# A two-layer graph network on one core: the loads, table stores and first splits ahead of the second product, put in another order

## The chip, the cores and the metric

The kernel runs on one core of one Trainium2 chip. The metric is the device time of one execution in microseconds; the median of three runs is quoted. Everything else is read from one profiled execution.

## The reference

```python
N, F = 4096, 128        # x: [N, F], adj: [N, N], symmetric pattern, non-negative
h = relu(layernorm(x))
d = 1 / sqrt(adj.sum(-1))
z = leaky_relu((d * (adj @ (d * h))) @ W1 + b1, 0.1)
dist = sqrt(max(sq_i + sq_j - 2 z z^T, 0) + 1e-10)
S = where(rank of exp(-dist / 2) in its row < 4, exp(-dist / 2), 0)
d2 = 1 / sqrt((S + adj).sum(-1))
x = x + (d2 * ((S + adj) @ (d2 * h))) @ W2 + b2
h = relu(layernorm(x))
x = x + h @ W_self.T + (adj @ h) @ W_neigh.T + b
```

The adjacency matrix, 64 MB, is multiplied three times. S has four entries in each row, so S @ (d2 * h) @ W2 is a sum of four gathered rows of a table d2 * (h @ W2).

## The kernel before, in words

Rows are kept in 32 tiles of 128, four tiles (U) to a group, eight groups (GROUPS). The adjacency is cut into 64 units of 1 MB (128 partitions x 4 x 512); a unit (g, j) is what group g needs of group j. The first product reads the matrix, transposes the units on VectorE and keeps them in HBM as `at`.

**Search.** Then, for each of 32 tiles, TensorE makes 4096 distances (`distances`, L1259), ScalarE brings them into one of four key buffers (`keys`, which are the four slots of `araw`), and VectorE finds the four best. Tiles go in quads. For three of each quad (`VIA`) VectorE reduces blocks of 64 to their maxima (L988), SyncE stores the keys in HBM (`keys_store`, L440), GpSimd gathers the four best blocks back (`read_blocks`, L501, the gathers at L511), and VectorE searches these candidates (L1010, L1012). The fourth is searched whole (L1001, L1003). GpSimd also adds the first layer's bias to `xs` (L535) between the gathers.

**Between search and second product.** The four values of a row go through a square root and exp (L1034 to L1038), and `dinv` is made of the new row sums (L1041). GpSimd decodes the block places into row indices (L567 to L576). VectorE scales `hw_sb`, the rows of h @ W2 (it lies in two slots of `tr`), by `dinv` into `gw` (`table_part`, L1048; it lies in `zt_lo`), and SyncE stores `gw` in HBM as the neighbour table (L476, four transfers of 512 KB in runs of 512 B). When it has landed (`table_out`), GpSimd gathers from it: 8 groups of 16 indirect transfers of 128 rows (`gather_group`, L578, L588), which go into `zt_lo`, over `gw`. Group g waits until VectorE has used group g-2 (`gath_used`).

**Second product.** It holds one group of accumulations at a time, eight units each. The units lie in a ring of eight places (`ring`, the same memory as the key buffers: two units in each key buffer), loaded by SyncE (`load_unit`, L418, the transfer at L428) as soon as TensorE has used the unit before in that place (`u_used`). Even units are multiplied as they are (`whole_unit`, L1294, 4 matmuls) by `ys` (`second_y`, L1044). Odd units are split: ScalarE casts them into a high part (`split_high`, L755, L761, in one of four places of `ring_hi`, the memory of `tr`), VectorE subtracts to get the low part (`split_low`, L1118, L1122), and TensorE runs three products of each block (L1289 to L1291) with the high and low parts of y, made by ScalarE (`y_hi`, L796) and VectorE (`second_y_low`, L1051). After a group, VectorE adds the gathered rows (`finish_second_a`, L1070, L1080), adds to x, takes the layer norm's statistics, and ScalarE and VectorE make and keep the next h (L781, L784, L1116). On VectorE these stand between the last split of group g+1 and the first of group g+2.

**Third product.** All units are split; group g needs all kept h. GpSimd adds the last bias (L603), which waits for `bias_in`.

The order on each engine is that of the code. The work around the change, on SyncE:

```python
            sp.wait_ge(x_b2, QUADS - 1)          # L462: seven bias additions of GpSimd
            sp.wait_ge(kept, 1)                  # L463: and the eighth
            sp.dma_start(bias[:], ...)           # L464
            for p in range(4):                   # L465
                ...                              # key buffer p stored and searched
                load_unit(0, 2 * p), load_unit(0, 2 * p + 1)
            sp.wait_ge(gw_ready, 1)              # L474
            ...                                  # four table stores, L476
```

Of the kernel before, what the change touches and what calls it, by code (L numbers as in the profile page):

```python
# [31 lines left out]
P = 128  # L32
QD = 4
R = 32
TILES = N // P
U = 4
GROUPS = TILES // U
# [10 lines left out]
QUADS = TILES // 4  # L48
# [3 lines left out]
DMA = 16  # L52


def gnn_kernel(nc, x, adj, W1, b1, W2, b2, W, b, out):
# [12 lines left out]
    table_v = table.rearrange("(q t s) f -> q s t f", q=QD, t=TILES)  # L68
# [3 lines left out]
    with ctx:  # L72
        places = {}

        def sb(name, shape, dt=F32):
            places[name] = -(-nc.sbuf_base // 32) * 32
            return ctx.enter_context(nc.sbuf_tensor(name, shape, dt))
# [4 lines left out]
        def sem(name):  # L82
            return ctx.enter_context(nc.semaphore(name))
# [23 lines left out]
        bias = sb("bias", [P, F])  # L107
# [65 lines left out]
        gw = units_z[1][:].rearrange("p i u (k f) -> p (i u k) f", f=F)  # L173
# [20 lines left out]
        bias_in = sem("bias_in")  # L194
# [42 lines left out]
        x_b2 = sem("x_b2")  # L237
# [20 lines left out]
        gw_ready = sem("gw_ready")  # L258
        table_out = sem("table_out")
# [10 lines left out]
        kept = sem("kept")  # L270
        last_bias = sem("last_bias")
        dinv_done = sem("dinv_done")
# [130 lines left out]
        def _(sp):  # L403
# [55 lines left out]
            with sp.Fori(1, QUADS) as quad:  # L459
                for p in range(VIA):  # L460
                    keys_store(quad, p)
            sp.wait_ge(x_b2, QUADS - 1)  # L462
            sp.wait_ge(kept, 1)  # L463
            sp.dma_start(bias[:], b.partition_broadcast(P)).then_inc(bias_in, DMA)  # L464
            for p in range(4):  # L465
                if p < VIA:
                    sp.wait_ge(keys_out[p], QUADS * 4 * DMA)
# [3 lines left out]
                for half in range(CHUNK_UNITS):  # L471
                    load_unit(0, p * CHUNK_UNITS + half)

            sp.wait_ge(gw_ready, 1)  # L474
            for q in range(QD):
                sp.dma_start(table_v[q], gw[R * q:R * q + R]).then_inc(table_out, DMA)  # L476

            with sp.Fori(1, GROUPS) as g2:
                for j in range(GROUPS):
# [10 lines left out]
        def _(gp):  # L490
# [99 lines left out]
                            in_offset=bass.IndirectOffsetOnAxis(ap=idx_st[:, i, u * TOPK + k:u * TOPK + k + 1], axis=0),  # L590
                            bounds_check=N - 1).then_inc(gath_in[i], DMA)

            gp.wait_ge(table_out, QD * DMA)
            for i in range(2):
                gather_group(i, i)
            with gp.Fori(1, GROUPS // 2) as pair:
# [9 lines left out]
        def _(act):  # L606
# [148 lines left out]
            def split_high(g2, j):  # L755

                place = split_place(g2, j)
                if g2 > 0:
                    act.wait_ge(u_used, used_before(g2, j))
                act.wait_ge(a_in[j], g2 * DMA + DMA)  # L760
                act.activation(ring_hi[:, place % TSLOTS], ring[:, j], ACT.Copy).then_inc(hi_done, 1)  # L761
# [27 lines left out]
                act.wait_ge(q_mm, g + GROUPS)  # L789
                act.activation(flat(t_st[:]), ps_t, ACT.Copy).then_inc(zt_ev, 1)  # L790

            act.wait_ge(dinv_done, 1)
            for g in range(1, GROUPS, 2):
                for u in range(U):
                    t = GROUPS * u + g
                    ins = act.activation(y_hi[:, t], hs[:, t], ACT.Identity, scale=dinv[:, t:t + 1])  # L796
                ins.then_inc(y_hi_done, 1)

            act.wait_ge(gw_ready, 1)
            for g in range(GROUPS):  # L800
                for j in range(1, GROUPS, 2):
                    split_high(g, j)
                    if g >= 1 and j == 3:
                        evacuate(g - 1, (g - 1) % 2, g * GROUPS, g - 1 + GROUPS)
                    if g >= 2 and j == 5:
                        transposed_second(g - 2)
                if g >= 1:
                    spread_second(g - 1)
                    normalize_second(g - 1)
# [28 lines left out]
        def _(v):  # L838
# [205 lines left out]
            def second_y(g):  # L1044
                v.tensor_tensor(ys_g[:, g], hs_g[:, g], dinv_g[:, g].unsqueeze(2).broadcast_to([P, U, F]), ALU.mult).then_inc(y_ready, 1)  # L1045

            def table_part(first, last):
                return v.tensor_tensor(gw[:, first:last], hw_sb[:, first:last],  # L1048
                                       dinv[:, first:last].unsqueeze(2).broadcast_to([P, last - first, F]), ALU.mult)

            def second_y_low(g):  # L1051
                v.wait_ge(y_hi_done, g // 2 + 1)
                for u in range(U):
                    t = GROUPS * u + g
                    ins = v.scalar_tensor_tensor(y_lo[:, t], hs[:, t], dinv[:, t:t + 1], y_hi[:, t].bitcast(F32), ALU.mult, ALU.subtract)
                ins.then_inc(y_lo_done, 1)

            second_y(0)
            v.wait_ge(hw_in, QD * DMA)
            table_part(0, TILES // 2)  # L1060
            second_y_low(1)
            table_part(TILES // 2, TILES).then_inc(gw_ready, 1)
            for g in range(2, GROUPS, 2):
                second_y(g)
                second_y_low(g + 1)

            base2 = count[0]
            PER_FINISH2 = TOPK - 1
# [49 lines left out]
            def split_low(g2, j):  # L1118

                place = split_place(g2, j)  # L1120
                v.wait_ge(hi_done, place + 1)
                v.tensor_tensor(ring_lo[:, j], ring[:, j], ring_hi[:, place % TSLOTS].bitcast(F32), ALU.subtract).then_inc(lo_done, 1)  # L1122
# [7 lines left out]

            for g in range(GROUPS):
                for j in range(1, GROUPS, 2):
                    split_low(g, j)
                if g >= 1:
                    finish_second_a(g - 1)
                    finish_second_b(g - 1)
                    if g >= 2:
                        finish_second_c(g - 2)
                    keep_low(g - 1)
# [255 lines left out]
```

## Time and profile before

| | us |
|---|---|
| median of 3 runs | 1203.1 (1202.9 to 1205.86) |
| the profiled execution | 1203.42 |
| its span, first to last instruction | 1201.3 |
| TensorE matmul busy | 943.6 (79%) |
| VectorE busy | 768.9 (64%) |
| GpSimd busy | 743.4 (62%) |
| ScalarE busy | 556.0 (46%) |
| granted TensorE clock, mean | 0.910 of full speed |

PE is TensorE's matmuls, PEld its weight loads, DVE is VectorE, ACT ScalarE, POOL GpSimd, SP SyncE; SPq and POOLq are the sequencers that issue DMAs. In lists of instructions and in the chain of work a row gives start, duration, engine, line, operation, output and input; what stands in brackets is the idle time before it and what ended that. The stage of interest lies between the last key stores (731 us) and the last gather (1004 us).

### The profile page before, as it was taken

Reading aid. Unit: us, or ns where it says so; the run is one execution under the profiler, and the core shown is the slowest. Engines: PE = TensorE matmul, PEld = TensorE weight load, DVE = VectorE, ACT = ScalarE, POOL = GpSimd, SP = SyncE. Lnnn points to the kernel's source line nnn. Section 1 sums busy time; section 2 is a strip of 40 time slices with the busy share of each in tenths; the row PEclk is TensorE's granted clock in tenths of the full one; section 3 lists DMA queues with packets and bytes.
Section 4 is the critical chain, followed back from the end, with each engine's and each line's share of the span. In section 5 each row is a group of like instructions: output and inputs, shape, how many; then the busy total and the mean of one; then the engine's idle time right before and its main releaser. Section 6 shows DMA issues by size and latency. Waiting matters only on the chain.

```text
span 1201.3 us, 12831 instructions
## 1 busy us (share of the span) xinstructions
PE 943.6 (79%) x3442; PEld 637.2 (53%) x3442; DVE 768.9 (64%) x855; ACT 556.0 (46%) x1154; POOL 743.4 (62%) x1089
## 2 busy tenths in 40 slices
PE   0136546757868877799999995698999985999998
PEld 0113222323334433488888884365666654788886
DVE  1544635455446655368999898736756665888884
ACT  2455343544602210266666664523343442676773
POOL 9999999999748784036555556387788875100000
PEclk9978668779879988899999998799999997999999
DMA  9999999999999999396666664998999983899992
GB/s 215 322 319 315 328 331 367 350 352 352 372 353 368 363 367 344 132 313 237 231 233 232 236 236 143 366 406 339 349 359 348 352 329 119 295 375 389 371 386 107
DMA packets 132617, 369.41 MB, mean 307 GB/s; under 512 B 44256, under 2 KB 69600, under 8 KB 108000
## 3 DMA queue, kind: packets, MB, share of 16 engines
q1 hardware_dynamic: 59872, 260.53, 56.1%
q0 software_dynamic: 63488, 104.23, 30.0%
q10 hardware_dynamic: 9216, 4.20, 1.3%
q8 instruction: 14, 0.23, 0.1%
q14 instruction: 27, 0.22, 0.1%
HBM read 244.78 MB, written 123.73 MB: 307 GB/s over the span
## 4 chain that ended last, share of the span: by engine, by line
PE 36%; POOL 13%; issue 8%; DMA 4%; DVE 3%; SPq 1%; ACT 1%; POOLq 0%; DVEq 0%; ACTq 0%
POOL zt_lo L588 11%; PE ps L1268 5%; PE ps L1271 5%; PE ps L1269 5%; PE ps L1270 5%; PE ps L1289 5%; PE ps L1290 5%; PE ps L1291 5%; DMA araw<-in_adj_dram 3%; POOL araw L375 1%; PE ps L1179 1%; SPq L476 1%; PE ps L1167 1%; DMA neighbour_table<-unit_zt_lo 1%; DVE out_t L1080 1%
## 5 line engine op out<-in xcount | busy, mean ns | idle before, releaser
L375 POOL DMA_DIRECT2D araw<-in_adj_dram x704 | 413.8, 597 | 44.5 <-DVE tr L861 28.9
L1122 DVE TENSOR_TENSOR araw_r<-araw,tr_r 128x2048 fp32r<-128x2048 f32 x96 | 217.4, 2295 | 69.1 <-ACT tr_r L761 69.0
L761 ACT ACTIVATE tr_r<-araw 128x2048 fp32r<-128x2048 f32 x96 | 181.3, 1910 | 79.7 <-PE ps L1291 37.8
L588 POOL DMA_INDIRECT zt_lo<-neighbour_table,idx_st x128 | 168.4, 1315 | 46.7 <-issue 40.1
L725 ACT ACTIVATE araw<-ps,nsq 128x1024 f32<-128x1024 f32 x128 | 143.0, 1117 | 80.3 <-PE ps L1271 80.3
L1179 PE MATMUL ps<-tr,ys 128*128 128x512 f32 x256 | 131.6, 665 | 26.6 <-DVE ys L868 22.2
L623 ACT ACTIVATE ps<-araw 128x256 f32<-128x256 f32 x304 | 111.3, 366 | 88.5 <-DMA araw<-in_adj_dram 84.0
L1298 PE MATMUL ps<-araw,ys 128*128 128x512 f32 x256 | 117.2, 601 | 18.2 <-DVE ys L1045 18.2
L861 DVE STREAM_TRANSPOSE tr<-araw 128x2048 f32<-128x2048 f32 x32 | 72.8, 2296 | 74.2 <-DMA araw<-in_adj_dram 67.0
L1289 PE MATMUL ps<-araw_r,zt_hi 128*128 128x512 f32 x256 | 103.3, 404 | 19.6 <-DVE araw_r L1122 19.6
L890 DVE TENSOR_REDUCE part<-araw 128x16 f32<-128x4096 f32 x13 | 57.4, 4416 | 87.6 <-DMA araw<-in_adj_dram 60.7
L988 DVE TENSOR_REDUCE bmax<-araw 128x64 f32<-128x4096 f32 x23 | 101.5, 4414 | 12.0 <-ACT araw L725 10.7
L1268 PE MATMUL ps<-sq_rows,pick 128*128 128x512 f32 x256 | 100.4, 392 | 2.9 <-ACT zs_lo L713 2.9
L1179 PEld LDWEIGHTS ps<-tr,ys 128*128 128x128 f32 x256 | 53.5, 217 | 91.4 <-issue 63.1
L1290 PE MATMUL ps<-tr_r,sq_rows 128*128 128x512 f32 x256 | 101.7, 397 | 0.0
L1291 PE MATMUL ps<-tr_r,zt_hi 128*128 128x512 f32 x256 | 101.6, 397 | 0.0
L1269 PE MATMUL ps<-zt_lo,zs_hi 128*128 128x512 f32 x256 | 100.1, 391 | 0.0
L1271 PE MATMUL ps<-zt_hi,zs_hi 128*128 128x512 f32 x256 | 100.1, 391 | 0.0
L1270 PE MATMUL ps<-zt_hi,zs_lo 128*128 128x512 f32 x256 | 100.1, 391 | 0.0
L511 POOL DMA_INDIRECT t_st<-keys_scratch,block_row x64 | 66.5, 1040 | 36.3 <-issue 25.1
L1298 PEld LDWEIGHTS ps<-araw,ys 128*128 128x128 f32 x256 | 48.6, 193 | 67.7 <-issue 65.8
L1205 PE MATMUL ps<-part,fold 128*128 128x16 f32 x64 | 14.1, 360 | 81.1 <-DVE part L890 81.1
(157 smaller groups left out, 1509.2 us busy)
## 6 DMA issues: line engine op xcount, KB each, us to landing
araw<-transposed SPq DMA_DIRECT2D x128, 1024.0 KB, 6.9
araw<-in_adj_dram POOLq DMA_DIRECT2D x704, 128.0 KB, 10.4
keys_scratch<-araw SPq DMA_DIRECT2D x96, 512.0 KB, 2.6
transposed<-tr SPq DMA_DIRECT2D x32, 1024.0 KB, 8.4
transposed<-unit_zt_hi SPq DMA_DIRECT2D x8, 1024.0 KB, 8.2
transposed<-unit_zt_lo SPq DMA_DIRECT2D x8, 1024.0 KB, 8.9
transposed<-unit_sq_rows SPq DMA_DIRECT2D x8, 1024.0 KB, 8.5
transposed<-araw SPq DMA_DIRECT2D x8, 1024.0 KB, 8.2
```

Of the source, the lines that this page charges most:

```text
L375: gp.dma_start(araw[R * q + first:R * q + R:SPREAD, place], adj_v[q, first:R:SPREAD, g // 2, g % 2, :, c]).then_inc(a_first_in[place], DMA)
L588: gp.indirect_dma_start(out=gath[:, i, u, k, :], out_offset=None, in_=table, in_offset=bass.IndirectOffsetOnAxis(ap=idx_st[:, i, u * TOPK ...
L761: act.activation(ring_hi[:, place % TSLOTS], ring[:, j], ACT.Copy).then_inc(hi_done, 1)
L1122: v.tensor_tensor(ring_lo[:, j], ring[:, j], ring_hi[:, place % TSLOTS].bitcast(F32), ALU.subtract).then_inc(lo_done, 1)
L1179: pe.matmul(acc[bank], ys[:, i * GROUPS + j], rhs[:, i], start=start and i == 0, stop=stop and i == U - 1)\
L1268: pe.matmul(ps[:, c], pick[:], sq, start=True, stop=False)
L1269: pe.matmul(ps[:, c], zs_hi[:, par], zl, start=False, stop=False)
L1270: pe.matmul(ps[:, c], zs_lo[:, par], zh, start=False, stop=False)
L1289: pe.matmul(acc[bank], hi[:, t], t_lo, start=j == 0 and i == 0, stop=False)
L1290: pe.matmul(acc[bank], lo[:, t], t_hi, start=False, stop=False)
L1291: ins = pe.matmul(acc[bank], hi[:, t], t_hi, start=False, stop=j == GROUPS - 1 and i == U - 1)
L1298: ins = pe.matmul(acc[bank], ys[:, i * GROUPS + j], ring[:, j, i], start=j == 0 and i == 0, stop=j == GROUPS - 1 and i == U - 1)
```

## The change

On SyncE the bias load with its two waits goes behind the table stores, so that the loads of the first eight units stand directly behind the key stores. The table is stored in two halves of 16 tiles, each after a signal of its own; GpSimd waits for all eight transfers. VectorE scales both halves one after the other; the low parts of y and the later even groups of `ys` are made inside the loop, each in front of the split that follows it. ScalarE splits the odd units 1 and 3 of group 0 between its `y_hi` groups, and waits for both table halves before the units 5 and 7, whose places in `ring_hi` hold `hw_sb`.

```diff
@@ SyncE
-            sp.wait_ge(x_b2, QUADS - 1)
-            sp.wait_ge(kept, 1)
-            sp.dma_start(bias[:], b.partition_broadcast(P)).then_inc(bias_in, DMA)
             for p in range(4):
...
-            sp.wait_ge(gw_ready, 1)
-            for q in range(QD):
-                sp.dma_start(table_v[q], gw[R * q:R * q + R]).then_inc(table_out, DMA)
+            for half in range(2):
+                sp.wait_ge(gw_ready, half + 1)
+                these = slice(half * TILES // 2, (half + 1) * TILES // 2)
+                for q in range(QD):
+                    sp.dma_start(table_v[q][:, these], gw[R * q:R * q + R, these]).then_inc(table_out, DMA)
+            sp.wait_ge(x_b2, QUADS - 1)
+            sp.wait_ge(kept, 1)
+            sp.dma_start(bias[:], b.partition_broadcast(P)).then_inc(bias_in, DMA)
@@ GpSimd
-            gp.wait_ge(table_out, QD * DMA)
+            gp.wait_ge(table_out, 2 * QD * DMA)
@@ ScalarE
-            act.wait_ge(dinv_done, 1)
-            for g in range(1, GROUPS, 2):
+            def second_y_high(g):
+
                 for u in range(U):
                     t = GROUPS * u + g
                     ins = act.activation(y_hi[:, t], hs[:, t], ACT.Identity, scale=dinv[:, t:t + 1])
                 ins.then_inc(y_hi_done, 1)
 
-            act.wait_ge(gw_ready, 1)
+            act.wait_ge(dinv_done, 1)
+            second_y_high(1)
+            split_high(0, 1)
+            second_y_high(3)
+            split_high(0, 3)
+            second_y_high(5)
+            second_y_high(7)
+            act.wait_ge(gw_ready, 2)
             for g in range(GROUPS):
                 for j in range(1, GROUPS, 2):
-                    split_high(g, j)
+                    if g >= 1 or j >= U:
+                        split_high(g, j)
@@ VectorE
             second_y(0)
             v.wait_ge(hw_in, QD * DMA)
-            table_part(0, TILES // 2)
-            second_y_low(1)
-            table_part(TILES // 2, TILES).then_inc(gw_ready, 1)
-            for g in range(2, GROUPS, 2):
-                second_y(g)
-                second_y_low(g + 1)
+            for half in range(2):
+                table_part(half * TILES // 2, (half + 1) * TILES // 2).then_inc(gw_ready, 1)
...
             for g in range(GROUPS):
                 for j in range(1, GROUPS, 2):
+                    if g == 0:
+                        second_y_low(j)
+                        if j + 1 < GROUPS:
+                            second_y(j + 1)
                     split_low(g, j)
```

## Rows read from the trace of the kernel before

**Rows 1.** Busy time by stretch: length, then each engine's busy us (instructions), clock, DMA share, GB/s
```profile
core 0: us, PE busy (x) PEld busy (x) DVE busy (x) ACT busy (x) POOL busy (x), PEclk, DMA share, GB/s
780.00:1000.00 220.00, 211.91 (x769) 136.47 (x768) 130.47 (x261) 83.86 (x89) 173.28 (x136) 0.98 0.93 347
```

**Rows 2.** The chain that ended last, 744 to 782 us: start, us, what
```profile
748.25 0.42 DVE m L1010
...
753.78 0.36 DVE dinv L1041
...
758.85 2.21 DVE unit_zt_lo L1048
...
773.40 6.27 DMA neighbour_table<-unit_zt_lo
...
779.80 0.21 POOL idx_st L584
```

**Rows 3.** The chain that ended last, 994 to 1024 us
```profile
998.74 5.50 DMA zt_lo<-neighbour_table,idx_st
```

**Rows 4.** Who waited for whom, 755 to 1040 us: total, times, longest
```profile
DVE out_t L1080 <- DMA zt_lo<-neighbour_table,idx_st: 40.9, 8, 10.7
...
ACT tr_r L761 <- DMA araw<-transposed: 24.8, 10, 4.2
```

**Rows 5.** Instructions of VectorE in order of time, 725 to 1050 us
```profile
774.36 2.29 DVE L1122 TENSOR_TENSOR araw_r<-araw,tr_r 128x2048 fp32r<-128x2048 f32 x1 [1.69 <-ACT tr_r L761]
...
810.15 1.12 DVE L1080 SCALAR_TENSOR_TENSOR out_t<-zt_lo,vals,ps 128x128 f32<-128x128 f32 x4 [2.42 <-DMA zt_lo<-neighbour_table,idx_st]
...
836.49 1.12 DVE L1080 SCALAR_TENSOR_TENSOR out_t<-zt_lo,vals,ps 128x128 f32<-128x128 f32 x4 [4.85 <-DMA zt_lo<-neighbour_table,idx_st]
...
1004.33 1.12 DVE L1080 SCALAR_TENSOR_TENSOR out_t<-zt_lo,vals,ps 128x128 f32<-128x128 f32 x4 [10.73 <-DMA zt_lo<-neighbour_table,idx_st]
```

**Rows 6.** Instructions of TensorE in order of time, 735 to 860 us
```profile
768.42 0.77 PE L1289 MATMUL ps<-araw_r,ys_r 128*128 128x512 f32 x1 [7.39 <-DVE araw_r L1122]
...
824.83 0.79 PE L1289 MATMUL ps<-araw_r,ys_r 128*128 128x512 f32 x1 [3.33 <-DVE araw_r L1122]
```

**Rows 7.** DMA issues of SyncE in order of time, 725 to 800 us
```profile
725.75 5.68 SPq L446 DMA_DIRECT2D keys_scratch<-araw  x4
...
747.84 5.37 SPq L428 DMA_DIRECT2D araw<-transposed  x8
...
776.26 22.47 SPq L428 DMA_DIRECT2D araw<-transposed  x10
```

**Rows 8.** Busy time by shorter stretches, columns as in rows 1
```profile
518.00:526.00 8.00, 8.00 (x37) 6.63 (x36) 4.95 (x4) 5.61 (x7) 4.34 (x5) 1.00 1.14 200
...
749.00:751.00 2.00, 0.00 (x0) 0.00 (x0) 0.64 (x3) 0.70 (x2) 1.35 (x5) 0.50 0.71 122
...
773.00:779.00 6.00, 6.00 (x21) 3.65 (x20) 2.29 (x1) 1.33 (x1) 0.00 (x0) 0.99 0.90 213
753.00:769.00 16.00, 6.29 (x10) 2.75 (x11) 15.18 (x25) 10.80 (x21) 7.53 (x9) 0.71 1.01 424
```

**Rows 9.** The candidate gathers: the last one, and landing times from 738 to 748 us
```profile
744.75 1.01 POOL L511 DMA_INDIRECT out_t<-keys_scratch,block_row  x1 [0.30 <-issue]
...
DMA to landing us min/median/max: 2.4/2.5/2.7
```

**Rows 10.** The table gathers: group, forms, and starts of GpSimd's index copies
```profile
L588 POOL DMA_INDIRECT zt_lo<-neighbour_table,idx_st x128 | 168.4, 1315 | 46.7 <-issue 40.1
...
L588 POOL DMA_INDIRECT zt_lo<-neighbour_table,idx_st x128: 1006/1014/3102, 780.8 to 998.7; - x128
...
805.26 0.21 POOL L584 COPY idx_st<-idx 128x16 uint32<-128x16 uint32 x1
...
833.85 0.20 POOL L584 COPY idx_st<-idx 128x16 uint32 x1
...
886.02 2.25 POOL L584 COPY idx_st<-idx 128x16 uint32 x1
...
916.35 0.21 POOL L584 COPY idx_st<-idx 128x16 uint32 x1
```

## The prediction
> **What bounds the kernel now.** I read first the busy times of the engines by stretch, to find what is busy in the second product, behind the stage that the edits touch. From 780 to 1000 us TensorE is busy 211.9 of 220, GpSimd 173.3 and the DMA engines 93% [rows 1]. Both look like the limit there, so the chain of work that ended last decides. It runs from dinv (L1041, start 753.78) over the scaling of the neighbour table on VectorE (L1048, twice), the four table stores on SyncE's queue (L476) and their landing at 779.67 into the first index copy of GpSimd at 779.80 [rows 2]. From there it stays on GpSimd's 128 gathers until the last one, issued at 998.74, lands 5.50 us later at 1004.24 [rows 3]. Only then does it pass through VectorE's sums (L1080) to the last product. The waits of the second product say the same: VectorE waited for gathered rows in all 8 groups, 40.9 us in total [rows 4]. Group 7's wait, 10.73 us, is the longest [rows 5]. TensorE's stall at 824.83 (3.33 us) is the echo of it: the split that it waits for stands behind those sums on VectorE [rows 6].
>
> So the question of this change is: when has the table landed, and does GpSimd keep its pace from there? The stores are late for a reason that SyncE's queue shows. SyncE finished the key stores at 731.4, then waited for GpSimd's last bias addition, issued the bias load, and only from 747.84 on the eight loads of 1 MB [rows 7]. These fill the DMA engines at 424 GB/s from 753 to 769 us; behind them the stores run at 213 GB/s [rows 8]. The table was scaled at 761.06, but landed only 18.6 us later [rows 2].
>
> **Part 1: loads as key buffers come free.** The bias load and its two waits move behind the table stores. Nothing needs that bias before the additions at L603, far later. SyncE then reaches the loads at 731.4: units 0 to 3 at once (the maxima of their key buffers are done by 730.3), units 4 and 5 when VectorE's reduction of the third buffer ends, at 735.7 (by the order of its instructions), units 6 and 7 at 747.4 as before, since the search of the fourth buffer ends there. In the trace of before the DMA engines had little to do between 735 and 749, so this traffic is taken out of the way: 6 of 8 units are in by about 733.5 + 6 x 1.049 MB / 424 GB/s (14.8) = 748.3, the last two by about 753.3. The table stores then find an empty queue.
>
> What it costs: the candidate gathers of the last keys (L511) now run beside loads. The last is issued at 744.75, ends its issue at 745.76, and lands about 2.5 us later [rows 9]; VectorE takes it up at 748.25 without slack [rows 2]. So each microsecond of delay goes into dinv in full. The nearest rows are the table gathers, which land beside the same kind of loads: from the end of the last issue of groups 0 and 1 (805.26 and 833.85, less a tenth) to VectorE's start at 810.15 and 836.49 it is 4.9 and 2.65 us [rows 5, 10]; of group 7 it is 4.5 us (5.50 less the issue of 1.01) [rows 3]. Against 2.5 that is a delay of 0.15 to 2.4 us; I take 1.3, the middle. From above, if the gather had to let all six loads pass, it would land at 748.3 + 2.5 = 750.8, a delay of 2.5. A gain is excluded, since no load ran there before.
> The Trainium skill (DMA: Bandwidth & Descriptors, Queues, rings and completion order) says that each DMA engine takes turns between its queues packet by packet. By that rule the gathers do not wait for the whole backlog of SyncE's queue, and the delay stays under the 2.5 us; the rows of groups 0 and 1 agree.
>
> **Part 2: table in halves, scaled back to back.** VectorE's order after dinv (754.13) was second_y(0), half 0, four low parts (1.39 us), half 1. The low parts move behind, so half 0 is ready at 757.46 as before and half 1 at 757.46 + 2.3 = 759.8 instead of 761.07. The stores grow from 4 to 8 with the same runs of 512 B, so the same packets. An idle queue's data starts some 1.9 us after its issue: the loads issued at 747.84 moved 0.24 MB from 749 to 751 (122 GB/s at a DMA share of 0.71), so they began between 749.4 and 750.4 [rows 7, 8]. Then 2.10 MB. At 205 GB/s (200 GB/s in 518 to 526, where the same table's source was read back in runs of 512 B, and 213 in the pure store stretch [rows 8]) it takes 10.2 us. As the fast end I take 9.0: the 8.4 MB of loads, at 424 GB/s from about 750.2, end near 770.0, so the stores had 9.7 us behind them and a little beside them. So the landing is at 757.5 + 1.9 + 10.2 = 769.6 for an unchanged dinv, or 768.4 at the fast end and 771.1 at 180 GB/s. Half 1 is ready at 759.8, inside the 5 us that half 0 takes, so no gap. Against 779.67 that is 10.1 us (8.6 to 11.3); less the 1.3 of part 1: **8.8 us earlier**.
>
> **Part 3: two odd units split first, low parts inside the loop.** ScalarE casts unit 1 after 4 of its 16 activations and needs no table signal for it: done by about 758.5, long before VectorE asks. VectorE: dinv at 755.4, second_y 0.9, table 4.7, low 1.2, second_y 0.65, split 2.25 = 765.1; before it was 768.32. TensorE, whose first odd unit began at 768.42 [rows 6], begins 3.3 us earlier. The stall at 824.83 also goes: VectorE's sums of group 0 follow the landing (810.15 - 8.8 = 801.3), the split that TensorE then needs comes 14.7 us after their start (824.8 - 810.15), thus at 816, and TensorE arrives at 820.9 - 3.3 = 817.6. With 1.3 us less at the lower clock (six matmuls at 0.43 instead of 0.23 us) TensorE is 7.9 us ahead. That keeps it in front of the gathers' demand.
>
> SyncE, too, is free 8.8 us earlier for the loads of group 1, first issued at 776.26 [rows 7]. GpSimd's waits for gath_used have room: gather group 2 starts at 833.85 while the sums of group 0 ended near 814.8; both move together.
>
> What is given back: gathers that meet a split on VectorE (L1122) take longer. Their shortest is 1.006 us, the median 1.014, the longest 3.10; the excess of all (168.4 - 128 x 1.006 = 39.6 us) [rows 10] over some 31 splits is 1.28 us for one split. In the trace no split of group 0 fell on a gather: the last ran from 774.36 to 776.65 [rows 5], the first gather began at 780.77. Now the gathers start near 772, and units 5 and 7 are split until 773.1 and 776.5. One to two splits more lie on GpSimd's path: 0 to 4 us, I take 1.3.
> The Trainium skill (GPSIMD Engine Reference, Specifications) says that GpSimd shares its SBUF interfaces with VectorE and contends with instructions that have two SBUF inputs. This speaks against the change, since table halves, low parts and splits are all of that kind. The table halves meet only the index decoding, which has until 770.9 to finish and ended near 761.2.
>
> **Sum.** Table landing 10.1 earlier, 1.3 for the candidates, 1.3 for the split: the last gather lands 7.5 us earlier, and everything behind it with it, since group 7's wait on VectorE was 10.73 us. VectorE reaches that point some 8 us earlier as well. Profiled execution: 1203.4 - 7.5 = 1195.9; against the median of the runs, 1203.1, this is **1195.6 us**. Its own range is 1193 to 1198.
>
> **Rivals.**
> - *More gain* (1192.0): stores at the fast end (11.3), candidates delayed 0.2, no new collision: 11.1 us. For it speaks that no other traffic runs beside the stores; against it the 200 and 213 GB/s. Chance 0.12.
> - *The product is the bound* (1199.8): only TensorE's 3.3 us at the first odd unit reach the end. It would hold if the stall at 824.83 came from ScalarE's late loads (L761 waited for DMA 24.8 us in ten pieces [rows 4]). Against it, VectorE waited for gathers in every group. Chance 0.13.
> - *Nothing, or slower: GpSimd gives it back.* A group of gathers takes 27.5 us on average (779.80 to 999.75, in 8), the longest 30.3 (886.02 to 916.35) [rows 2, 3, 10], depending on how VectorE's splits fall on it. With splits freed from waits for data, they may fall worse. The point from which it decides: a mean of 28.6 us eats the 8.8 us (1203.1). At 29.4, the mean of that longest and of the one before 833.85 (28.6), it is 8 x 1.9 = 15.2 us against 8.8: **1209.5, slower**. For it speaks the spread of the groups (25.5 to 30.3); against it that VectorE's work per group is unchanged. Chance of no change 0.12, of slower 0.06.
> - *The change doesn't do what it says*: the second half's stores or the last two loads hold the first half. Units 6 and 7 go out at 747.4 and are in 4 us before the first store, so this is inside the ranges.
>
> **How the numbers follow.** Forecast 0.57, more gain 0.12, product 0.13, no change 0.12, slower 0.06. The measurement tells about 0.3%, 3.6 us, from nothing: 1199.5 and below is faster. The product case lies on that line; I count most of it as faster. Faster 0.78, same 0.16, slower 0.06. The range 1190.5 to 1200.5 leaves out slower and no change, 0.18, and takes in the ends of the store rate.
>
> **What would show it.** Loads at L428 from 731.5 on, six of eight before 737. dinv between 754.3 and 756.6. Eight stores from 758 on, table landed and first index copy near 771 (767 to 773). First odd unit on TensorE near 765. Last gather's landing at 996 to 998, with VectorE's wait there still 8 us or more. Wrong would be: dinv later than 758, stores under 180 GB/s, gather groups above 28.5 us, or a TensorE stall where there was none. If the wait of VectorE for group 7 is gone, gathers no longer bound the end.

## The result, and the profile after

| | us |
|---|---|
| changed kernel, median of 20 | 1200.93 (1197.15 to 1204.65) |
| kernel before, median of 20 on the same chip | 1203.68 (1198.83 to 1207.46) |
| ratio | 0.9973, interval 0.9961 to 0.9985 |
| forecast | 1195.6, range 1190.5 to 1200.5 |

The change gains 0.27%, 3 us, where 7.5 us were forecast. The profiled execution of the changed kernel took 1201.45 us, with a span of 1199.4; the one before 1203.42 and 1201.3. In the changed kernel the lines moved: L1001 is L1011, L1041 is L1051, L1048 is L1058, L1080 is L1086, L1122 is L1128, L584 is L586, L588 is L590.

The chain that ended last in the changed kernel, 740 to 800 us (start, duration, what), answers to [rows 2]:

```profile
743.76 6.39 DMA out_t<-keys_scratch,block_row
750.24 0.44 DVE m L1020
...
755.80 0.36 DVE dinv L1051
...
766.26 4.65 DMA neighbour_table<-unit_zt_lo
...
771.03 2.75 POOL idx_st L586
```

The table lands at 770.91, 8.7 us earlier, where 8.8 were forecast. That is luck in part: the search happened to be 1.06 us earlier in this execution (its last full pass began at 737.32, before at 738.38). Against that pass, dinv is 3.1 us later, 18.48 us behind it instead of 15.40. VectorE now waits 2.96 us for the last candidates, which land 6.39 us after the start of their issue; before it was about 2.5 [rows 9].

SyncE's issues, in order of time, answer to [rows 7]: the eight loads begin at 730.66, the stores are eight, and the next loads go out at 769.25 instead of 776.26.

```profile
730.66 16.52 SPq L428 DMA_DIRECT2D araw<-transposed  x8
759.51 7.91 SPq L475 DMA_DIRECT2D neighbour_table<-unit_zt_lo  x8
767.52 1.38 SPq L478 DMA_DIRECT2D bias<-in_L_gnn_b_dram  x1
769.25 38.30 SPq L428 DMA_DIRECT2D araw<-transposed  x14
```

Where the 8.7 us went is seen on GpSimd. First its instructions in the changed kernel, then VectorE's splits of the same stretch, the first two (units 5 and 7) with what stands before them:

```profile
771.03 2.74 POOL L586 COPY idx_st<-idx 128x16 uint32<-128x16 uint32 x1 [8.24 <-DMA neighbour_table<-unit_zt_lo]
774.55 3.43 POOL L590 DMA_INDIRECT zt_lo<-neighbour_table,idx_st  x1 [0.78 <-POOL idx_st L586]
778.28 1.02 POOL L590 DMA_INDIRECT zt_lo<-neighbour_table,idx_st  x1 [0.30 <-issue]
...
780.92 2.58 POOL L590 DMA_INDIRECT zt_lo<-neighbour_table,idx_st  x1 [0.30 <-issue]
...
787.75 2.65 POOL L590 DMA_INDIRECT zt_lo<-neighbour_table,idx_st  x1 [0.30 <-issue]
...
793.33 2.84 POOL L590 DMA_INDIRECT zt_lo<-neighbour_table,idx_st  x1 [0.30 <-issue]
...
799.11 2.41 POOL L590 DMA_INDIRECT zt_lo<-neighbour_table,idx_st  x1 [0.30 <-issue]
...
804.16 0.21 POOL L586 COPY idx_st<-idx 128x16 uint32<-128x16 uint32 x1
```
```profile
770.84 0.68 DVE L1055 TENSOR_TENSOR ys<-hs,dinv 128x512 f32<-128x512 f32 x1
771.44 2.27 DVE L1128 TENSOR_TENSOR araw_r<-araw,tr_r 128x2048 fp32r<-128x2048 f32 x1
773.64 1.12 DVE L1065 SCALAR_TENSOR_TENSOR hs_r<-hs,dinv,ys_r 128x128 fp32r<-128x128 f32 x4
774.69 2.28 DVE L1128 TENSOR_TENSOR araw_r<-araw,tr_r 128x2048 fp32r<-128x2048 f32 x1
780.32 2.29 DVE L1128 TENSOR_TENSOR araw_r<-araw,tr_r 128x2048 fp32r<-128x2048 f32 x1 [3.35 <-ACT tr_r L763]
787.22 2.29 DVE L1128 TENSOR_TENSOR araw_r<-araw,tr_r 128x2048 fp32r<-128x2048 f32 x1 [4.61 <-ACT tr_r L763]
793.00 2.29 DVE L1128 TENSOR_TENSOR araw_r<-araw,tr_r 128x2048 fp32r<-128x2048 f32 x1 [3.48 <-ACT tr_r L763]
798.34 2.29 DVE L1128 TENSOR_TENSOR araw_r<-araw,tr_r 128x2048 fp32r<-128x2048 f32 x1 [3.05 <-ACT tr_r L763]
```

Each of the six splits has a long row of GpSimd beside it: the index copy (2.74 instead of 0.20 us) and five gathers of 2.41 to 3.43 us, where 1.01 is the undisturbed duration. A gather that begins while a split runs ends 0.9 us after the split's end: the one of 787.75 at 790.40, the split at 789.51. The first two rows are longer than that: the copy began at 771.03, during the scaling of `ys`, and the first gather at 774.55, during the low parts of y, before their splits had begun. VectorE ran on without a gap, and both were held until the split that followed had ended (the gather then took another 1.0 us). Group 0 of the gathers thus lasts from 771.03 to 804.16, 33.1 us; before it lasted 25.5 us and met three splits, those at 787.90, 793.99 and 799.46.

The account against the search's last pass, changed less before: dinv +3.1; from dinv to the first index copy -10.8 (15.2 instead of 26.0 us); the 128 gathers +6.8, of which group 0 alone is +7.7; the last landing +0.2; from there to the end -0.2. Sum -0.9, and -1.1 of the earlier search makes the -1.9 us between the two profiles. VectorE still waits at group 7, 10.99 us against 10.73 [rows 5], so the gathers still set the end.

### The profile page after: what moved, and what is told of

Read it like the earlier page. It is cut to its first block and busy times, and to the rows that moved or that the text cites. A ratio compares the mean times of both kernels' runs of the same rounds, so it can differ in the third digit from the quotient of the medians.

```text
span 1199.4 us, 12835 instructions
## 1 busy us (share of the span) xinstructions
PE 940.3 (78%) x3442; PEld 633.6 (53%) x3442; DVE 768.2 (64%) x855; ACT 555.5 (46%) x1154; POOL 750.1 (63%) x1089
## 5 line engine op out<-in xcount | busy, mean ns | idle before, releaser
L1128 DVE TENSOR_TENSOR araw_r<-araw,tr_r 128x2048 fp32r<-128x2048 f32 x96 | 216.9, 2293 | 59.6 <-ACT tr_r L763 59.5
L590 POOL DMA_INDIRECT zt_lo<-neighbour_table,idx_st x128 | 174.3, 1362 | 48.3 <-issue 41.7
L1189 PE MATMUL ps<-tr,ys 128*128 128x512 f32 x256 | 135.4, 681 | 31.4 <-DVE ys L878 24.7
L1308 PE MATMUL ps<-araw,ys 128*128 128x512 f32 x256 | 117.3, 601 | 21.3 <-DVE ys L1055 21.3
L513 POOL DMA_INDIRECT t_st<-keys_scratch,block_row x64 | 66.7, 1042 | 37.2 <-issue 25.1
```

Of the source, the lines that this page charges most:

```text
L590: gp.indirect_dma_start(out=gath[:, i, u, k, :], out_offset=None, in_=table, in_offset=bass.IndirectOffsetOnAxis(ap=idx_st[:, i, u * TOPK ...
L1189: pe.matmul(acc[bank], ys[:, i * GROUPS + j], rhs[:, i], start=start and i == 0, stop=stop and i == U - 1)\
L1308: ins = pe.matmul(acc[bank], ys[:, i * GROUPS + j], ring[:, j, i], start=j == 0 and i == 0, stop=j == GROUPS - 1 and i == U - 1)
```

## The experiments

Theory A: the gathers set the end, and an early table is spent on meetings of gathers with splits. Theory B: DMA traffic makes the gathers long. Theory C: TensorE's product sets the end. The times are medians; each ratio is to the kernel before on the same chip. All differ from the full change unless said otherwise.

| kernel | time | ratio (interval) | search pass to dinv | dinv to first copy | group 0 | groups 1 to 7, mean |
|---|---|---|---|---|---|---|
| before | 1203.68 | 1 | 15.4 | 26.0 | 25.5 | 27.8 |
| full change | 1200.93 | 0.9973 (0.9961 to 0.9985) | 18.5 | 15.2 | 33.1 | 27.7 |
| e1 loads only | 1203.12 | 0.9964 (0.9944 to 0.9983) | 18.0 | 19.1 | 28.1 | 27.9 |
| e2 order only | 1205.68 | 0.9985 (0.9964 to 1.0006) | 15.4 | 25.7 | 25.8 | 28.1 |
| e3 late third | 1200.74 | 0.9956 (0.9939 to 0.9974) | 15.6 | 15.1 | 33.6 | 28.0 |
| e4 six whole | 1195.72 | 0.9913 (0.9884 to 0.9942) | 18.0 | 14.8 | 22.8 | 28.2 |
| e5 four pieces | 1186.98 | 0.9859 (0.9816 to 0.9903) | 17.8 | 15.1 | 29.5 | 25.2 |
| e6 no copy | 1194.09 | 0.9922 (0.9901 to 0.9943) | 17.7 | | | |
| e7 three edits | 1183.88 | 0.9849 (0.9802 to 0.9896) | 15.9 | | | |
| e8 before, four pieces | 1190.39 | 0.9884 (0.984 to 0.9929) | 15.4 | 26.0 | 24.1 | 25.1 |
| e9 full change again | 1201.22 | 0.9972 (0.9954 to 0.999) | 17.7 | 14.9 | 33.0 | 27.4 |
| e10 hold | 1202.16 | 0.9983 (0.9969 to 0.9997) | 17.8 | 21.3 | 28.8 | 27.4 |
| e11 two pieces | 1187.96 | 0.9868 (0.9839 to 0.9897) | 17.9 | 14.8 | 29.2 | 26.1 |
| e12 three edits again | 1183.73 | 0.9832 (0.9803 to 0.9862) | 15.9 | | | |

The four columns on the right are of one profiled execution each: the start of VectorE's full search pass to that of the reciprocal that makes dinv, from there to GpSimd's first index copy, from that to the second, and the seventh part of the time from the second to the end of the last gather's issue. e6, e7 and e12 have no index copies. The medians of e1 to e4, e5 to e8 and e9 to e12 come from three sets; the kernel before had 1206.53, 1204.16 and 1204.88 there.

### e1: the loads alone

```diff
 # the kernel before, on SyncE
-            sp.wait_ge(x_b2, QUADS - 1)
-            sp.wait_ge(kept, 1)
-            sp.dma_start(bias[:], b.partition_broadcast(P)).then_inc(bias_in, DMA)
             for p in range(4):
 ...
                 sp.dma_start(table_v[q], gw[R * q:R * q + R]).then_inc(table_out, DMA)
+            sp.wait_ge(x_b2, QUADS - 1)
+            sp.wait_ge(kept, 1)
+            sp.dma_start(bias[:], b.partition_broadcast(P)).then_inc(bias_in, DMA)
```

> Part 1 alone: on SyncE the bias load goes behind the table stores, all else as before (one table signal, four stores, low parts between the halves, splits after the table). Theory A (the gathers set the end; an early table makes them meet more splits on VectorE): dinv comes 3 us later against the search than before (candidates beside loads), the table lands about 3.5 to 4.5 us earlier, gather group 0 lasts 27 to 30 us instead of 25.5; net 0 to 3 us faster than before. Theory B (DMA traffic beside the gathers, not VectorE, makes group 0 long): group 0 lasts 33 us as in the full change, net about 3 us slower than before. Theory C (TensorE's product sets the end): TensorE gains nothing, so 2 to 3 us slower by the late dinv.

Ratio 0.9964, 4.3 us faster than before, a little more than A had it. dinv is 2.6 us later against the search, the first copy comes 6.9 us earlier after dinv, and group 0 lasts 28.1 us. B's 33 us and C's loss are not there. This one move gives what the full change gives: the two intervals overlap nearly whole.

### e2: the order alone

```diff
 # the full change, on SyncE
+            sp.wait_ge(x_b2, QUADS - 1)
+            sp.wait_ge(kept, 1)
+            sp.dma_start(bias[:], b.partition_broadcast(P)).then_inc(bias_in, DMA)
             for p in range(4):
 ...
-            sp.wait_ge(x_b2, QUADS - 1)
-            sp.wait_ge(kept, 1)
-            sp.dma_start(bias[:], b.partition_broadcast(P)).then_inc(bias_in, DMA)
```

> Parts 2 and 3 without part 1: halves, order on VectorE and ScalarE as changed, but SyncE waits for the bias additions before the eight loads, as before. A: dinv as before, loads fill the DMA engines until about 770, the table lands within 1 us of before (779.7), group 0 of the gathers 25 to 28 us; the time is that of before within 1.5 us. C: the first odd unit waits for its load anyway, but where it is split 2 to 4 us earlier TensorE's lead reaches the end: 2 to 4 us faster than before.

Ratio 0.9985, not told from no change. TensorE's first odd unit began 3.00 us after the even one ended, not 7.39 as in [rows 6]. In the profiles nothing of that reached the end: from the search's last pass to the end of the span it is 463.6 us here and 462.9 before. The medians alone leave room for C's 2 to 4 us (the interval reaches from 4.3 us faster to 0.7 slower); e6 decides more clearly. The first copy was 25.7 us behind dinv, as before: the halves are worth nothing while the stores stand behind eight loads.

### e3: the third buffer's loads behind the candidates

```diff
                     sp.wait_ge(block_maxima, (QUADS - 1) * VIA + p + 1)
+                    if p == VIA - 1:
+                        sp.wait_ge(cand_in[p], QUADS * CAND)
```

> The full change, but the two loads into the third key buffer wait until the last candidate gathers have landed. A and the reading of the candidates: only four loads (until about 744) lie beside the gathers, VectorE's 2.96 us wait at the last candidates falls under 0.7, dinv comes 2.4 to 3.1 us earlier against the search; the table stores start behind four loads that end near 758, so the table lands 1.5 to 3 us earlier; end 1.5 to 3 us earlier than the full change (about 1198.5). If the wait for candidates has another cause than the loads, dinv stays 18.5 us behind the search's last pass and the time is unchanged or up to 1 us longer.

The candidates' delay goes from 3.1 to 0.2 us: dinv is 15.6 us behind the search pass. That it came from the loads is shown. The end gains less than that, if anything: 0.9956 against 0.9973 and 0.9972, 2 us with intervals that overlap. Group 0 of the gathers lasts 33.6 us, again beside six splits.

### e4: six splits taken off VectorE

```diff
 # split_low, VectorE
-                v.tensor_tensor(ring_lo[:, j], ring[:, j], ring_hi[...], ALU.subtract).then_inc(lo_done, 1)
+                if g2 == 1 or (g2 == 0 and j > U):
+                    c = (g2 * TSLOTS + j // 2) % 8
+                    v.tensor_copy(bm8[:, c:c + 1], bmax[:, 0:1]).then_inc(lo_done, 1)
+                else:
+                    v.tensor_tensor(ring_lo[:, j], ring[:, j], ring_hi[...], ALU.subtract).then_inc(lo_done, 1)
 # group_second, TensorE
+                    if j % 2 and isinstance(g, int) and (g == 1 or j > U):
+                        pe.wait_ge(lo_done, g * TSLOTS + (j // 2 + 1))
+                        whole_unit(g, j, i, j - 1)
-                    if j % 2:
+                    elif j % 2:
```

> The full change, but VectorE makes no low parts for units 5 and 7 of group 0 and the four odd units of group 1 (an operation of one column signals in their place), and TensorE multiplies these six units whole, with the y of their even neighbour: the contribution of those six units is left wrong, the number of bytes, loads, casts and gathers is kept. A: gather group 0 meets no split and lasts 22 to 23.5 us instead of 33.1 (the index copy 0.2 instead of 2.74), its first copy still near 771; the later groups keep their 27.5. The last gather lands 8 to 10 us earlier and the end follows by 6 to 10 us. B (DMA traffic): group 0 stays at 30 us or more, end within 2 us of the full change. C: group 0 shortens but the end stays within 2 us.

The copy and the first gathers of this kernel:

```profile
772.68 0.99 POOL L586 COPY idx_st<-idx 128x16 uint32<-128x16 uint32 x1 [7.79 <-DMA neighbour_table<-unit_zt_lo]
774.44 1.28 POOL L590 DMA_INDIRECT zt_lo<-neighbour_table,idx_st  x1 [0.78 <-POOL idx_st L586]
776.03 1.01 POOL L590 DMA_INDIRECT zt_lo<-neighbour_table,idx_st  x1 [0.30 <-issue]
...
794.44 1.01 POOL L590 DMA_INDIRECT zt_lo<-neighbour_table,idx_st  x1 [0.30 <-issue]
795.45 0.21 POOL L586 COPY idx_st<-idx 128x16 uint32<-128x16 uint32 x1
```

Every gather of group 0 from the second on takes 1.01 us, beside nearly the same loads as in the full change (392 and 404 GB/s from 775 to 795 us). Group 0 falls from 33.1 to 22.8 us, and the kernel is 0.6% (7.2 us) faster than the full change. B falls. The end by itself does not tell gathers from TensorE here, because the six units leave out their low parts and spare TensorE 48 matmuls too; but VectorE still waited 10.1 us for the gathered rows of group 7, so the gathers set the end. The later groups do not keep their pace: here they take 28.2 us on average, the longest 29.7. VectorE no longer waits for gathered rows in groups 0 to 5, and its splits come more singly, as TensorE frees their places, each with a gather beside it. That this is what slows the later groups is argued from the trace, not shown by a run.

### e5 and e11: the split in four and in two pieces

```diff
 # split_low, VectorE; e11 has 2 for 4
-                v.tensor_tensor(ring_lo[:, j], ring[:, j], ring_hi[...], ALU.subtract).then_inc(lo_done, 1)
+                pieces = 4 if g2 <= GROUPS else 1
+                wide_u = U // pieces
+                for i in range(pieces):
+                    us = slice(i * wide_u, (i + 1) * wide_u)
+                    ins = v.tensor_tensor(ring_lo[:, j, us], ring[:, j, us], ring_hi[..., us], ALU.subtract)
+                ins.then_inc(lo_done, 1)
```

> The full change, but VectorE's subtraction for the low part of a unit in the second product (2048 columns, 2.29 us) is made in four pieces of 512 columns. Theory A1 (a gather that begins while a two-input instruction of VectorE runs waits for the end of that instruction and then runs its 0.9 to 1.0 us): the wait falls from up to 2.4 to under 0.7 us, the mean gather from 1.36 to 1.1 us, gather group 0 from 33 to 23 to 26 us, the others from 27.5 to 23 to 25; TensorE (27 us per group) becomes the bound, the last gather lands at least 8 us earlier, the end comes 6 to 12 us earlier. Theory A2 (GpSimd is shut out as long as VectorE works on such data, whatever the pieces): groups within 1 us of the full change, each split 0.1 to 0.3 us longer, end 0 to 2 us later. Theory B (DMA traffic): no change in the gathers.

> The full change with VectorE's subtractions of the second product in two pieces of 1024 columns (1.15 us). Wait for the end of the running instruction: single gathers in the later groups last at most about 2.0 us (3.1 with 2048 columns, 1.5 with 512), groups 25 to 26 us, the end between the full change and four pieces: 6 to 10 us faster than the full change. If the gain of four pieces comes from something else than the length of one instruction, two pieces give the same as four or nothing.

The same work in smaller instructions is 1.1% faster than the full change: 0.9859 with four pieces, 0.9868 with two. Both are some 13 us faster, more than the 6 to 12 and 6 to 10 expected. VectorE itself gets slower by it, 2.50 us for a unit instead of 2.29. A stretch of three splits in a row, gathers and pieces of e5:

```profile
869.81 1.49 POOL L590 DMA_INDIRECT zt_lo<-neighbour_table,idx_st  x1 [0.30 <-issue]
871.60 1.50 POOL L590 DMA_INDIRECT zt_lo<-neighbour_table,idx_st  x1 [0.30 <-issue]
873.41 1.50 POOL L590 DMA_INDIRECT zt_lo<-neighbour_table,idx_st  x1 [0.30 <-issue]
...
869.72 7.42 DVE L1132 TENSOR_TENSOR araw_r<-araw,tr_r 128x512 fp32r<-128x512 f32 x12 [1.11 <-ACT tr_r L763]
```

Behind the first one, a gather takes up to 1.53 us beside pieces of 512 columns, up to 2.03 (most often 1.97) beside pieces of 1024, and 1.89 to 3.10 beside whole splits. So a gather that begins during a piece or a split waits for the end of that one instruction and gets in before the next: there A1 holds and A2 falls. Two pieces gave nearly what four give, and by my expectation that would speak for another cause than the length of the instruction. The medians cannot decide it, since the two intervals overlap; the durations of the single gathers do. A new bound may be why four pieces bring no more: VectorE waited for gathered rows 16.9 us in all with two pieces and 5.6 with four (40.9 in [rows 4]). No run tests that.

One thing of A1 did not come true: group 0 of e5 took 29.5 us, not 23 to 26. Its first copy and first gather are still long:

```profile
772.60 3.49 POOL L586 COPY idx_st<-idx 128x16 uint32<-128x16 uint32 x1 [8.11 <-DMA neighbour_table<-unit_zt_lo]
776.86 3.63 POOL L590 DMA_INDIRECT zt_lo<-neighbour_table,idx_st  x1 [0.78 <-POOL idx_st L586]
780.80 1.02 POOL L590 DMA_INDIRECT zt_lo<-neighbour_table,idx_st  x1 [0.30 <-issue]
```

The copy ends with the fourth piece at 776.03, the gather 1.0 us after the next unit's fourth piece at 779.49. There VectorE runs low parts, y and pieces without a wait between them. e11 has the same (3.39 and 3.49 us), and so have the first two rows of the full change above. Even in e4, without the splits, the copy was held from 772.68 until the low parts and `ys` had ended (773.61). These rows look as A2 has it. Why GpSimd does not get in between those instructions, and does between pieces later, stays open.

### e8: four pieces on the kernel before

```diff
 # the kernel before, split_low as in e5
```

> The kernel before, only with VectorE's subtractions of the second product in four pieces. A1: gather groups of 23 to 25 us from the same start (780), end 5 to 12 us faster than before, and since the table still lands at 779.7 the gap to the same edit on the full change shows what the earlier table is worth when gathers do not collide: 5 to 9 us. A2: within 1 us of before, or up to 2 us slower.

0.9884, 14 us faster than before (5 to 12 expected): more than the change itself brings, by one edit of VectorE's instruction length. Against e5 the earlier table is worth 0.25%, 3 us, less than the 5 to 9 expected, and with overlapping intervals not told from nothing: e5's table lands 8.5 us earlier against the search, but its group 0 takes 29.5 us and this one's 24.1.

### e6: gathers without the index copy

```diff
-                gp.tensor_copy(idx_st[:, i].rearrange("p (u k) -> p u k", u=U), src).then_inc(idx_ready, 1)
-                wait_alone(gp, idx_ready, g + 1)
 ...
-                            in_offset=bass.IndirectOffsetOnAxis(ap=idx_st[:, i, u * TOPK + k:u * TOPK + k + 1], axis=0),
+                            in_offset=bass.IndirectOffsetOnAxis(ap=idx[:, GROUPS * u + g, k:k + 1], axis=0),
 # the loop over the groups written out
```

> The full change, but the gathers take their indices from the index tile itself, written out for all 8 groups, without the copy of a group's indices and its wait. A group loses the copy (0.2 us alone, 2.74 where it meets a split) and the 0.8 us until its first gather, 0.7 us per group and about 2.5 more in group 0. If gathers set the end: 5 to 8 us faster than the full change. If a lead of the gathers is eaten by collisions with isolated splits (what the later groups of the run with six whole units suggest, 29.5 us instead of 27.5): 1 to 4 us faster. Theory C (TensorE sets the end): within 1 us.

0.9922, 6 us faster than the full change, inside "5 to 8 if gathers set the end". C, which allowed 1 us, falls: this edit touches GpSimd alone.

### e10 beside e9: the gathers held back

```diff
             gp.wait_ge(table_out, 2 * QD * DMA)
+            gp.wait_ge(lo_done, TSLOTS)
```

> The full change once more, beside the next three on one chip: ratio to before 0.9973 by the first measurement, gather group 0 at 33 us again if its six splits are the cause, dinv 18 to 18.5 us after the search's last pass begins.

> The full change, but GpSimd's first gather also waits until VectorE has made the low part of unit 7 of group 0, so the gathers begin 6 us later (near 777 instead of 771). Theory A (the early start is spent on waiting for splits): group 0 meets four splits instead of six, lasts 27 to 29 us instead of 33, and the end is 0 to 2.5 us later than the full change, less than the 6 us of the hold. If group 0 were long for a reason that sits in the gathers or in the DMA traffic, the end is 5 to 6 us later.

The hold moved the first copy from 14.9 to 21.3 us behind dinv, 6.4 us later. It met four splits instead of six, group 0 took 28.8 instead of 33.0 us, and the median rose by 0.9 us. So of the first 6.4 us of the earlier start the full change keeps about 1; the intervals overlap, and a loss of up to some 4 us fits, but not one of 5 to 6. The full change measured again gives 0.9972 and a group 0 of 33.0 us, as expected; dinv came 17.7 us behind the search pass, a little earlier than the 18 to 18.5 expected.

### e7 and e12: three edits together

The full change with e3's wait, e5's four pieces and e6's gathers.

> Full change with the third buffer's loads held until the candidates are in, subtractions in four pieces for the second product, and gathers without the copy. A1: gathers leave the path; TensorE's second product (27.1 us per group) and VectorE's sums set the end, 12 to 18 us faster than the full change (1183 to 1189). A2: 4 to 7 us faster than the full change, by the other two edits alone.

> The version with the third buffer's loads held, four pieces and no index copy, once more beside the full change: 0.985 of before, 14 to 17 us faster than the full change.

0.9849 and 0.9832, 20 to 21 us faster than before, 15 and 17.5 us faster than the full change. This version beats both kernels. GpSimd is off the path: VectorE waits for gathered rows only twice, 4.2 us in all in e12. Behind its first odd unit TensorE runs the second product of e12 with one stall of 0.35 us and stops only at the seam to the third product, where it waits for VectorE's splits:

```profile
819.31 0.50 PE L1297 MATMUL ps<-araw_r,ys_r 128*128 128x512 f32 x1 [0.35 <-DVE araw_r L1125]
...
980.96 0.47 PE L1297 MATMUL ps<-araw_r,zt_hi 128*128 128x512 f32 x1 [3.74 <-DVE araw_r L1125]
...
996.86 0.76 PE L1297 MATMUL ps<-araw_r,zt_hi 128*128 128x512 f32 x1 [3.63 <-DVE araw_r L1125]
...
1003.90 0.47 PE L1297 MATMUL ps<-araw_r,zt_hi 128*128 128x512 f32 x1 [1.58 <-DVE araw_r L1125]
```

## Why the prediction was wrong, point by point

**The bound** was right. The chain runs through table and gathers; e4 and e6, which change the gathers' pace, move the end, and e2, which brings TensorE forward without an earlier table, shows no gain clear of noise.

**The table's landing** was right in its parts. From dinv to landing 15.8 us were worked out (half 0 ready, 1.9 to first data, 10.2 for 2.1 MB), and it took 15.1. The stores ran at 224 GB/s, faster than the 205 taken and slower than the fast end (2.1 MB in 9.0 us, 233 GB/s):

```profile
761.00:769.00 8.00, 5.01 (x18) 2.97 (x17) 8.00 (x13) 7.18 (x11) 1.65 (x3) 0.96 0.94 224
```

(stretch, length, busy time of PE, PEld, DVE, ACT and POOL, clock, DMA share, GB/s).

**The candidates** were mis-sized: 1.3 us taken, 0.15 to 2.4 as bounds and 2.5 as the worst, 3.1 measured here and 2.3 to 2.6 in seven other profiles with the same loads (e1, e4 to e6, e9 to e11); e3 gives them back. The prediction also misread a row. The 2.5 us of [rows 9] run from the start of an issue, not from its end, so before the last candidates had landed at 747.3, 1.0 us before VectorE took them up. They landed 3.9 us later after their issue now, of which this slack absorbed 1.0. The bounds compared 4.9, 2.65 and 4.5 us from the end of an issue with those 2.5; that error is 1.0 us too, with the other sign, so the bounds stand. The bounds came from the table gathers, in traces where the DMA engines were at 93% and paused now and then. Here they were full from 735 to 753 us, and every candidate gather took 6.0 to 6.8 us from issue to landing (the changed kernel, 731 to 748 us):

```profile
DMA to landing us min/median/max: 6.0/6.4/6.8
```

The first of them, begun at 732.2 with 4 MB of loads ahead of it (10 us at 400 GB/s), took no longer than the last. They took their turn between the loads rather than queue behind them. The Trainium skill (DMA: Bandwidth & Descriptors, Queues, rings and completion order) says that a DMA engine takes turns between its queues, and the trace agrees. The 2.5 us of my worst case was no bound either: it had the six loads in by 748.3 at 424 GB/s, while the last key stores still ran until about 735 and the engines then moved 402 GB/s (735 to 745 us).

**What is given back** is the step that failed. The prediction said: "One to two splits more lie on GpSimd's path: 0 to 4 us, I take 1.3." It was three more, and 7.7 us. Over the undisturbed 0.20 and 1.01 us, units 5 and 7 cost 5.0 us (2.5 on the copy, 2.4 on the first gather), the fourth split of group 1 cost 1.4, and the three that group 0 had met before cost 5.0 instead of 3.7. Two errors made it up.
- The number. The sum counted units 5 and 7 and did not ask where the splits of group 1 go. But the same text said that SyncE is free 8.8 us earlier for the loads of group 1. These loads are what those splits wait for; they went out at 769.25, and all four splits came 6.5 to 7.6 us earlier, so group 0 lost none of its old meetings. The fourth, which before began just behind the group (805.45), now fell into it.
- The price of 1.28 us for a split was a mean over all of them, most of which run in rows behind VectorE's sums. There a gather gets in between two, and each later split costs 0.9 us. A split that stands alone costs 0.9 to 2.1 us, by how soon after its start a gather begins: 1.3, 0.9 and 1.5 in group 0 before, 1.6, 1.6, 1.8 and 1.4 now. The dearest two, units 5 and 7, do not stand alone. Low parts and `ys` run into them without a gap, and GpSimd was held through these too. The prediction had no term for that.

**The rival "GpSimd gives it back"** was the right mechanism with the wrong place. Its mean of 28.6 us per group for "nothing gained" was nearly met (28.3: 226.8 us in 8), but the excess was all in group 0 and followed from the order of the work, not from chance in how splits fall. I gave it 0.18 because "VectorE's work per group is unchanged"; that holds for the later groups (27.7 and 27.8 us), and the first one was not asked. The shortest group was 25.2 us (833.85 to 859.09), not the 25.5 named as the low end of the spread; nothing hangs on it.

**TensorE's part**: the first odd unit began 2.3 us earlier (766.15), where 3.3 were forecast, and 1.1 of the 2.3 is the earlier search; the stall at 824.83 was said to go and stayed (4.06 us at 822.81), since the gathers of group 0 ended only 1.1 us earlier than before and VectorE waited 7.42 us for them.

## What to carry to other kernels

When a step on the critical path is moved earlier, list every instruction of the other engines that will then run beside it, and move those that the same edit frees too. Where GpSimd's gathers run beside VectorE, price each meeting by the length of the single VectorE instruction, and look apart at stretches where VectorE runs different instructions without a gap; long two-input instructions cut into two to four pieces can be worth more than any reordering (14 us here, on the kernel before). And when the measured gain is small, compare the duration of the stage just behind the moved step: here the 10.8 us saved ahead of it were lost in the candidates (3.1) and in one group of gathers (7.7).

## What the runs showed of the hardware that I had not expected

- An indirect DMA's instruction on GpSimd, or a small copy there, that starts while VectorE runs a two-input subtraction waits for the end of that one instruction; a gather then takes its 0.9 to 1.0 us. It is 1.01 us alone, up to 1.53 beside 512-column pieces, 2.03 beside 1024 and 3.10 beside 2048. The Trainium skill (GPSIMD Engine Reference, Specifications) names contention with instructions of VectorE that have two SBUF inputs, and the trace agrees. The first copy and gather of group 0 do not fit and are open: in the full change (2.74 and 3.43 us), e5 and e11 (3.4 to 3.6 us, although the pieces are short) they were held through several instructions that follow each other without a gap.
- Candidate gathers beside full-rate loads took 6.0 to 6.8 us to land in the changed kernel, 2.4 to 2.7 without them [rows 9]. In five other profiles with the same loads (e5, e6, e9 to e11) those begun from 733 us on took 5.5 to 6.7 us. The time did not grow with the loads queued ahead.
- Parts of the program that no edit touches differ between executions: the start of the search's last pass ranges from 737.2 to 741.6 us in the profiles of this study. Differences under 3 us between two single profiles are read against a mark inside the trace, as was done here, not against its start.
